# Routing scores and the selected z kept in PSUM, and four weight differences formed later, in a fused conditional FFN

## The reference

```
W = L0_cond_weights[itok]                       # (64, 64, 64), one matrix per sample
y = einsum('bct,bcd->bdt', x, W)                # 64 samples of 64 x 1024
logits = y @ gate_w.T + expert_bias             # 4 experts
e = argmax(logits)                              # one expert per row
base = y @ W_up.T                               # 1024 x 1024
z = y @ lora_A[e].T                             # rank 8
out = x + base + z @ lora_B[e].T
```

## Time and profile before

| what | value |
|---|---|
| timed runs | 424.64, 424.82, 426.23 us; median 424.82 |
| span of the profiled execution, the only time of its own that the page gives | 422.5 us |
| chain that ended last | PE 91%, DVE 3%, ACT 1%, DMA 1%, POOL 1% |
| busy DVE / ACT / POOL | 280.2 / 146.0 / 137.2 us |
| granted TensorE clock | nine tenths or more of full speed in all 40 slices |

### The profile page before, as it was taken

One profiled execution on the slowest core, in us unless ns is written; L12 is line 12 of the kernel. 1 busy time (PEld: TensorE's weight loads), 2 busy tenths in 40 slices (PEclk: granted clock), 3 DMA queues, 4 the chain that ended last, 5 costly groups with the idle time before them and its releaser, 6 DMA issues.

```text
span 422.5 us, 8776 instructions
## 1 busy us (share of the span) xinstructions
PE 414.2 (98%) x3003; PEld 393.5 (93%) x3003; DVE 280.2 (66%) x605; ACT 146.0 (35%) x282; POOL 137.2 (32%) x123
## 2 busy tenths in 40 slices
PE   8998998999999999999999999999999999999997
PEld 7897998999999999999999999999999999999996
DVE  3999658686756567574676656565764746856684
ACT  5994222433324242242323332232432323323320
POOL 1688205507113080413505062040803226050530
PEclk9999999999999999999999999999999999999999
DMA  7900320503114032322025021140322212250102
GB/s 255 346 37 2 127 80 26 180 26 108 75 62 146 36 98 100 126 65 92 32 96 178 26 102 58 58 167 25 106 99 93 87 64 66 99 177 29 50 26 100
DMA packets 20991, 39.36 MB, mean 93 GB/s; under 512 B 7494, under 2 KB 7750, under 8 KB 20970
## 3 DMA queue, kind: packets, MB, share of 16 engines
q1 hardware_dynamic: 17600, 27.40, 18.2%
q10 hardware_dynamic: 3370, 11.69, 8.2%
HBM read 22.30 MB, written 16.78 MB: 92 GB/s over the span
## 4 chain that ended last, share of the span: by engine, by line
PE 91%; DVE 3%; ACT 1%; DMA 1%; SPq 1%; issue 1%; POOL 1%; ACTq 0%; POOLq 0%
PE bank_y L869 21%; PE bank_x L869 21%; PE y_ps L785 11%; PE bank_b L869 10%; PE bank_c L869 10%; PE bank_c L1071 5%; PE bank_b L1071 4%; PE bank_x L849 1%; DMA cond_pair<-in_L_cond_weights_dram 1%; PE bank_x L875 1%; PE bank_y L875 1%; PE bank_b L875 1%; PE bank_c L875 1%; PE y_ps L1147 1%; PE y_ps L803 1%
## 5 line engine op out<-in xcount | busy, mean ns | idle before, releaser
L524 ACT ACTIVATE a<-y_ps 128x512 f32<-128x512 f32 x49 | 29.3, 598 | 93.4 <-PE y_ps L785 93.4
L785 PE MATMUL y_ps<-cond_pair,x_sb 128*128 128x128 f32 x448 | 59.0, 274 | 0.0
L785 PEld LDWEIGHTS y_ps<-cond_pair,x_sb 128*128 128x128 f32 x448 | 54.7, 191 | 1.2
L869 PE MATMUL bank_y<-w_s,hl_s 128*128 128x292 f32 (+1 forms) x384 | 51.4, 289 | 0.0
L869 PE MATMUL bank_x<-w_a,hl_a 128*128 128x256 f32 (+1 forms) x384 | 50.9, 288 | 0.0
L869 PEld LDWEIGHTS bank_x<-w_a,hl_a 128*128 128x128 f32 x384 | 49.5, 188 | 0.3
L304 POOL TENSOR_TENSOR s_sum<-a 128x512 f32<-128x512 f32 x9 | 11.6, 1289 | 117.3 <-ACT a L524 115.2
L869 PEld LDWEIGHTS bank_y<-w_s,hl_s 128*128 128x128 f32 x384 | 49.2, 188 | 0.1
L869 PE MATMUL bank_b<-w_s,hl_s 128*128 128x512 f32 x192 | 47.9, 398 | 0.0
L869 PE MATMUL bank_y<-w_a,hl_a 128*128 128x292 f32 x360 | 47.7, 288 | 0.0
L869 PEld LDWEIGHTS bank_y<-w_a,hl_a 128*128 128x128 f32 x360 | 46.6, 188 | 0.3
(11 more groups left out here) (187 smaller groups left out, 648.1 us busy)
## 6 DMA issues: line engine op xcount, KB each, us to landing
out_dram<-x_sb SPq DMA_DIRECT2D x63, 256.0 KB, 2.0
x_sb<-in_x_dram ACTq DMA_DIRECT2D x22, 512.0 KB, 3.5
x_sb<-in_x_dram SPq DMA_DIRECT2D x10, 512.0 KB, 3.3
w_raw<-in_L_ffn_W_up_dram SPq DMA_DIRECT2D x8, 512.0 KB, 5.5
cond_pair<-in_L_cond_weights_dram SPq DMA_DIRECT2D x64, 16.0 KB, 2.2
out_dram<-x_sb SPq DMA_DIRECT2D x2, 128.0 KB, 2.0
router_sb<-in_L_ffn_lora_A_dram ACTq DMA_DIRECT2D x1, 128.0 KB
lora_b_sb<-in_L_ffn_lora_B_dram SPq DMA_DIRECT2D x1, 128.0 KB, 5.2
```

What stands on the lines that cost most here:

```text
L524: act.activation(to[:, :], y_ps[:, h, :], ACT.Copy).then_inc(y_summed, 1)
L785: mm = pe.matmul(y_ps[:, h, k * P:(k + 1) * P], x_sb[:, 2 * par + t, (h * KH + k) * P:(h * KH + k + 1) * P], cond_pair[:, 2 * par + t, :], ...
L869: mm = pe.matmul(dst, hl[op][:, a, k, :], w[:, b, k, cols], start=(fresh and k == 0 and a + b == 0), stop=(k == KH - 1 and a == 1), skip_g ...
```

## The change

scores and z_sel are no SBUF tiles any more. They are columns 256 to 291 and 292 to 323 of the PSUM bank whose product gave the scores: score writes over its own input. A filler tile of z_sel's size keeps the addresses in SBUF. route gets the parity `par` of the block, to find the bank. On POOL, form_fine 5 and 7 stay at the end of `one` but wait for step 28 of the routing (the end of block 1's second route), and 6 and 4 move behind block 2's sums and wait for u2_out 3. ACT's round_fine go to block 2: 5 and 7 behind round_even_a22, 6 and 4 behind round_a11. DVE's low_fine 5 and 7 stay in place, 6 and 4 go behind block 2's second route.

```diff
-        z_sel = sb("z_sel", [P, ER], fp32)
+        sb("gap_i", [P, ER], fp32)
-        scores = sb("scores", [P, GC], fp32)
@@ POOL
             def form_fine(n, a, b, after):
-                pool.wait_ge(fine_sum, after) if after else pool.wait_ge(rebuilt, 4)
+                if after:
+                    pool.wait_ge(fine_sum, after)
                 pool.tensor_tensor(FINE_SUM[n], a, b, ALU.subtract).then_inc(fine_sum, 1)
+
+            def form_first_fine():
+                pool.wait_ge(rebuilt, 4)
+                pool.wait_ge(route_step, ROUTE_STEPS * 4)
+                form_fine(5, REBUILT[0, 1], REBUILT[0, 0], 0)
+                form_fine(7, REBUILT[1, 1], REBUILT[0, 1], 1)
+
+            def form_last_fine():
+                pool.wait_ge(u2_out, 3)
+                form_fine(6, REBUILT[1, 1], FINE_SUM[5], 2)
+                form_fine(4, REBUILT[1, 0], FINE_SUM[6], 3)
@@ POOL, one: after add_s3
-                form_fine(5, REBUILT[0, 1], REBUILT[0, 0], 0)
-                form_fine(7, REBUILT[1, 1], REBUILT[0, 1], 1)
-                form_fine(6, REBUILT[1, 1], FINE_SUM[5], 2)
-                form_fine(4, REBUILT[1, 0], FINE_SUM[6], 3)
+                form_first_fine()
@@ POOL, even: after add_s3
+                if isinstance(g, int) and g == 0:
+                    form_last_fine()
@@ ACT, one: between move_z(q, 1, 1) and move_y(q + 1, 1, 1, a22_even)
-                round_fine(5)
-                round_fine(7)
-                round_fine(6)
-                act.wait_ge(product_done["a22"], 2)
-                act.wait_ge(rebuilt, 4)
-                round_fine(4)
@@ ACT, even
                 round_even_a22(q, g)
+                if isinstance(g, int) and g == 0:
+                    round_fine(5)
+                    round_fine(7)
                 move_z(q, 0, 0, bank_c[:, 0, :])
                 move_y(q + 1, 0, 0, a11)
                 round_a11(q + 1, True)
+                if isinstance(g, int) and g == 0:
+                    act.wait_ge(product_done["a22"], 2)
+                    act.wait_ge(rebuilt, 4)
+                    round_fine(6)
+                    round_fine(4)
                 act.wait_ge(low["s4"], q + 1)
                 move_y(q + 1, 0, 1, a12)
@@ DVE
+            def scores_of(bank):
+                return bank[:, 0, QUARTER:QUARTER + GC]
+
+            def z_sel_of(bank):
+                return bank[:, 0, QUARTER + GC:QUARTER + GC + ER]
+
             def score(bank, addend):
-                dve.tensor_tensor(scores[:, :], bank[:, 0, QUARTER:QUARTER + GC], addend[:, :], ALU.add)\
-                   .then_inc(route_step, 1)
+                dve.tensor_tensor(scores_of(bank), scores_of(bank), addend[:, :], ALU.add).then_inc(route_step, 1)
...
-            def route(q, t, used=True):
+            def route(q, par, t, used=True):
                 n = 2 * q + t
+                bank = chains[par if t else 1 - par]
...
@@ DVE, even
                 if isinstance(g, int) and g == 0:
-                    for n in FINE_AT:
-                        low_fine(n)
+                    low_fine(5)
+                    low_fine(7)
                 low_even_a22(g)
                 low_operand(dve, "a12", a12, q + 1)
                 after_p7(q, 0)
-                route(q, 1)
+                route(q, 0, 1)
+                if isinstance(g, int) and g == 0:
+                    low_fine(6)
+                    low_fine(4)
                 after_delta12(q, 0)
```

More of the change, by code:

```diff
@@ L1213, in low_gate_difference, with find_best, rank_best @@
                                   ALU.subtract).then_inc(gate_diff_low, 1)
+            def scores_of(bank):
+                return bank[:, 0, QUARTER:QUARTER + GC]
+            def z_sel_of(bank):
+                return bank[:, 0, QUARTER + GC:QUARTER + GC + ER]
             def score(bank, addend):
-                dve.tensor_tensor(scores[:, :], bank[:, 0, QUARTER:QUARTER + GC], addend[:, :], ALU.add)\
-                   .then_inc(route_step, 1)
-            def find_best(n):
+                dve.tensor_tensor(scores_of(bank), scores_of(bank), addend[:, :], ALU.add).then_inc(route_step, 1)
+            def find_best(n, bank):
                 dve.wait_ge(route_step, ROUTE_STEPS * n + 1)
-                dve.tensor_reduce(best[:, :], scores[:, 0:E], AX.X, ALU.max).then_inc(route_step, 1)
-            def rank_best(n):
+                dve.tensor_reduce(best[:, :], scores_of(bank)[:, 0:E], AX.X, ALU.max).then_inc(route_step, 1)
+            def rank_best(n, bank):
                 dve.wait_ge(route_step, ROUTE_STEPS * n + 2)
-                dve.scalar_tensor_tensor(out=ranks[:, :], in0=scores[:, 0:E], scalar=best[:, 0:1], in1=rank_w[:, :],
+                dve.scalar_tensor_tensor(out=ranks[:, :], in0=scores_of(bank)[:, 0:E], scalar=best[:, 0:1],
+                                         in1=rank_w[:, :],
                                          op0=ALU.is_equal, op1=ALU.mult).then_inc(route_step, 1)
@@ L1230, in find_first, with select_z, high_z @@
                 dve.tensor_reduce(first[:, :], ranks[:, :], AX.X, ALU.max).then_inc(route_step, 1)
-            def select_z(n):
+            def select_z(n, bank):
                 dve.wait_ge(route_step, ROUTE_STEPS * n + 4)
                 dve.scalar_tensor_tensor(
-                    out=z_sel[:, :].rearrange("p (e r) -> p e r", e=E),
+                    out=z_sel_of(bank).rearrange("p (e r) -> p e r", e=E),
                     in0=ranks[:, :].unsqueeze(2).to_broadcast([P, E, R]), scalar=first[:, 0:1],
-                    in1=scores[:, E:GC].rearrange("p (e r) -> p e r", e=E),
+                    in1=scores_of(bank)[:, E:GC].rearrange("p (e r) -> p e r", e=E),
                     op0=ALU.is_equal, op1=ALU.mult).then_inc(route_step, 1)
             def twice(z):
-                return z[:, :].unsqueeze(1).to_broadcast([P, 2, ER])
-            def high_z(n, used):
+                return z.unsqueeze(1).to_broadcast([P, 2, ER])
+            def high_z(n, bank, used):
                 dve.wait_ge(route_step, ROUTE_STEPS * n + 5)
@@ L1246, in high_z, with low_z @@
                     dve.wait_ge(z_turned, n)
-                dve.tensor_copy(z_parts[:, 0:4:2, :].bitcast(fp32r), twice(z_sel)).then_inc(route_step, 1)
-            def low_z(n):
+                dve.tensor_copy(z_parts[:, 0:4:2, :].bitcast(fp32r), twice(z_sel_of(bank))).then_inc(route_step, 1)
+            def low_z(n, bank):
                 dve.wait_ge(route_step, ROUTE_STEPS * n + 6)
-                dve.tensor_tensor(z_parts[:, 1:4:2, :], twice(z_sel), z_parts[:, 0:4:2, :], ALU.subtract)\
+                dve.tensor_tensor(z_parts[:, 1:4:2, :], twice(z_sel_of(bank)), z_parts[:, 0:4:2, :], ALU.subtract)\
                    .then_inc(route_step, 1)
-            def route(q, t, used=True):
+            def route(q, par, t, used=True):
                 n = 2 * q + t
-                find_best(n)
-                rank_best(n)
+                bank = chains[par if t else 1 - par]
+                find_best(n, bank)
+                rank_best(n, bank)
                 find_first(n)
-                select_z(n)
-                high_z(n, used or t)
-                low_z(n)
+                select_z(n, bank)
+                high_z(n, bank, used or t)
+                low_z(n, bank)
             def add_pair(bank, par, t, half):
@@ L1281, in after_p2 @@
                 score_p2(q, par)
-                route(q, 0, used)
+                route(q, par, 0, used)
             def after_p4(q, par):
@@ L1363, in _ @@
             score_p2(0, 0)
-            route(0, 0, False)
+            route(0, 0, 0, False)
             low_sum(dve, 1, 3)
@@ L1370, in _ @@
             after_delta11(0, 0)
-            route(0, 1)
+            route(0, 0, 1)
             after_p5(0, 0)
@@ L1408, in one @@
                 after_p7(q, 1)
-                route(q, 1)
+                route(q, 1, 1)
                 after_delta12(q, 1)
@@ L1473, in odd @@
                 if closing:
-                    route(q, 0)
+                    route(q, 1, 0)
                     low_operand(dve, "s4", a12, q)
```

## The result

| | before | changed |
|---|---|---|
| median | 424.73 us (6 runs) | 423.22 us (6 runs) |
| ratio changed / before | | 0.9946, 95% interval 0.992 to 0.9972 |
| the same pair, timed again in five rounds | 424.95 us (12 runs) | 422.13 us (6 runs) |
| ratio | | 0.9931, 0.9911 to 0.9952 |
| span and time of the profiled execution | 422.5 us (span) | 422.3 us, 424.8 us |

The first median of the changed kernel includes one slow execution of 828.57 us, which the ratio leaves out; without it the median is 422.77 us. So the change is worth 2.3 us (1.2 to 3.4) in the first comparison and 2.9 us (2.0 to 3.8) in the second. 422.0 us, or 0.9933, was forecast.

A forecast was written before the change was run, and what follows sets the result against it. PE, busy 98% of the 422.5 us span, bounds the kernel; only its idle time can be bought back. 1.0 + 1.29 + 0.57 = 2.86 us off 424.82 gives 422.0 us, range 421.4 to 423.2.

The forecast's parts named there:

- Sum: Whole kernel: 1.0 + 1.29 + 0.57 = 2.86 us gained, the 2.3 us offset between span and timed median staying.
- A: Turn of z in block 0's first tile, at 38.35 us; PE idled 0.93 us for z_parts; gain 1.0 us.
- Rival 1: Block 0: POOL's lock only changes victims, s1's product or second turn waits; A worth 0 to 0.4 us; chance 0.17.
- B: Turn of z, block 1's second tile (73.04 us): PSUM scores or the moved differences alone would cure it; gain 1.29 us.
- C: Block 2's s2 product, at 81.16 us, 0.41 us late for hl_s; earlier a22_even copy gains 0.57 us, 0.8 us slack.
- PSUM operands cost nothing: Score to low_z in each route: six steps on PSUM cost 0.01 us each, 0.06 us a route, inside the slack.
- Rival 3: Between score and turn in all 32 routes: short PSUM-fed DVE steps are dear, 425.5 or 447 us; chance 0.05.
- Hidden work: Block 2: forms, roundings and low_fine moved there are hidden in idle time of POOL, ACT and DVE; cost 0.
- A reading: Routing steps' medians of 195 to 252 ns were said to show 30 of the routes clear of POOL's hold-up.
- Rival 2: A PSUM operand does not spare the steps: A stays, B and C go, gain 1.86 us, 423.0 us; chance 0.08.

The follow-up runs named there:

- low order: Changed kernel with DVE's low_sum(1,1) ahead of low_sum(4,3), and low a11 only behind block 0's second route; ratio to the kernel before 0.9931.
- Forms late: Changed kernel, but POOL's four differences all behind block 1's second route and ACT's roundings ahead of a22_even's copy as before; ratio to the kernel before 1.0023.
- PSUM only: Changed kernel with the four differences put back as before on POOL, ACT and DVE, scores and z_sel in PSUM; ratio to the kernel before 0.9944.

## Why the prediction was right

Forecast 422.0 us, a ratio of 0.9933; measured 0.9946 and 0.9931. By its steps:

- **Sum.** 2.86 us forecast, 3.00 in the middle stretch. The offset between span and timed median was taken as fixed at 2.3. It is not: over the executions on record it goes from 1.8 to 2.3 us for the kernel before, from 1.8 to 2.9 for the changed one and from 2.5 to 2.7 for low order. The span's opening and tail vary by 3.0 and 1.2 us besides, and the spread of 0.2 us that the prediction allowed covers neither. The first comparison gave 2.3 us and the second 2.9; their intervals overlap, so this may be noise, of the ends among others.
- **A, forecast 1.0.** From the first score to delta12 of block 1 the changed kernel takes 36.36 us, the one before 37.36: 1.00. That it is so near is partly luck. The turn gained 1.08 (1.09 forecast). The waits behind the turn were hidden too, which was held for an upper bound and put at 0.2; they were worth 0.31, as the s4 product follows the turn by 0.03 us and not 0.34. Against that stand 0.28 us of wait for low_sum(1,1), where 0 to 0.1 was forecast, and 0.13 us between s1's start and the a22 product, which no term held: 1.08 + 0.31 - 0.28 - 0.13 is 0.98, and 0.02 lies elsewhere. The chain on DVE came as worked out: low_sum(1,1) ended 6.47 us after the score, inside the forecast's 6.4 to 6.6. It was PE that came sooner: unhindered, in low order, it starts s1 6.40 us after the score, where the forecast had 6.7. Rival 1 had the right mechanism and too high a price: it took 0.41 and not 0.6 to 1.0. Two further rows of the kernel before on which these differences rest, the s4 product and the a22 product:

```profile
38.69 2.97 PE L869 MATMUL bank_c<-w_s,hl_s 128*128 128x512 f32 x12
...
44.73 3.11 PE L869 MATMUL bank_x<-w_a,hl_a 128*128 128x256 f32 x24
```

- **B, forecast 1.29.** Measured 1.29, and cured by either half, as said.
- **C, forecast 0.57.** 3.60 us between a12 and s2 became 3.02: 0.58. Forms late measures the slack there: its copy is 3.4 us late, and s2 follows a12 (75.94) by 5.55 us instead of 3.02, so 2.5 came through and 0.8 to 0.9 was absorbed; 0.8 was forecast.
- **Rest.** 0.13 us of the 3.00 is in none of the three: 0.03 between B and C, and 0.10 from block 2's s2 to the last turn. Not looked into.
- **PSUM operands cost nothing, forecast 0.06 us a route.** From best to low_z a route takes 1.18 us between starts (44.67 to 45.85) where it took 1.14 (42.65 to 43.79). Rival 3 is out. By the figures of the Trainium skill ("VectorE: DVE Perf Modes", section "The TRN2 errata") the route would be some 0.32 us longer, an estimate; the measured 0.04 us decides against that.
- **Hidden work.** No step of the moved work showed on PE.
- **A reading.** The medians alone show that at least half of the routes are undisturbed, not that 30 are. What shows 30 is that only two turns waited, and that the 32 ranks were busy 8.7 us together: 30 of 0.22 and the two of 0.89 and 1.09.

Rival 2 (A stays) is out by the 0.22 us of the ranks in the middle of POOL's forms in PSUM only.

## What to carry to other kernels

Look for small vector instructions on the critical path beside a busy GpSimd: a 0.2 us step with two SBUF operands can cost 1.2 us, and putting one operand in PSUM, where it came from anyway, frees it without moving any work. The waiting does not vanish from the kernel, it passes to the next instruction with two SBUF operands, so look at what is queued there and order it by who needs it first. When a change is worth 3 us in 420, compare stretches between landmarks that both traces have: two profiles of the changed kernel agree there to 0.03 us, while its spans went from 419.0 to 422.3 us.

## What the runs showed that was not expected

The cast that makes z_parts had a median of 195 ns with both ends in SBUF and has 224 ns from PSUM; it is the only step of the route that grew by more than 10 ns. Before, it was also the one step with a single input that POOL held up (1203 ns at place A; at B, where it started just as POOL changed instruction, 0.20 us), while the reduction to `first`, a single input too, took 0.16 us in both routes. The Trainium skill ("SBUF — State Buffer", section "Who interferes with whom") lets copies and casts within SBUF use the shared pair, and reductions not; 1203 ns and 0.16 us fit.

One transfer that came 1.3 us late in the opening cost 3.0 us in one profile, as PE's granted clock then stood at 1.2 GHz (0.50 from 17.5 to 20.9 us) and the products behind it waited in turn. In another the same transfer was 0.7 us late, the clock stayed at 1.00, and it cost 0.7.
